# Two graph and two expert layers on one core: table work of the prologue split between VectorE and GpSimd, the count table cleared by ScalarE, weights loaded inside the first sums, narrow one-hots for the counted groups

## The chip, the cores and the metric

One core of a Trainium2 chip runs the whole program in one launch. The metric is the device time in microseconds (us); lower is better. Engines are named as the profile names them: PE (TensorE), DVE (VectorE), ACT (ScalarE), POOL (GpSimd), SP (SyncE, which only issues transfers here).

## The reference, cut to what matters

```python
n    = layernorm(x, eps=1e-5)                               # 3125 nodes x 256
# graph part of layer 0
msg  = concat(n[src], edge_attr_64) @ W_message              # 50,000 edges, 256 + 64 -> 256
agg  = segment_sum(msg, dst, 3125)
h    = layernorm(relu(agg) + n)
h    = mlp_with_skips(h, W0, W1, W2)
x    = x + layernorm(n + h)
# then: top-2 of 16 experts, a graph layer of neighbour means with top-32 of 256 kept, top-2 of 8 experts
```

The edges are sorted by `dst`, and `dst` is crowded at low nodes: about a third of the edges end in the first 350 nodes. The product with `W_message` is linear, so the kernel sums the raw rows per node first (256 features and 64 edge features) and multiplies by the weights afterwards.

## The kernel before

**Prologue** (up to the first `end_step()`, a barrier of all engines). The 3125 x 256 input comes in five pieces of five 128-row tiles (`X`); DVE takes statistics of each (L398, L402), inverts the deviation (L435, L437), ACT writes the normalized rows `NR` (L343), and SP stores them to memory as `n_rows` (L290), from where they are gathered later. The edge lists come in as `srci` and `dsti`, 98 groups of 512 edges, one group to a partition. DVE casts them to float (L406, L407) behind the third piece's statistics. When the fifth piece's statistics are done (`if p == IT`), DVE finds the smallest and largest node of each group and, for the first 33 groups, of each 128 edges (L411 to L429). `ends` holds three columns per group: first node, range, and the span of the 128-edge parts. PE turns `ends` into rows; DVE reads off two flags, `mixed_flag` and `order_flag`, which choose between a general path and the ordered path that this input takes. For the 33 dense groups ("counted" groups) DVE also makes the tables `low_i`, `high_i`, `low_f`, `rel_f`, `at_f` (L430 to L451), which PE turns into `lo_tab` and `at_tab`. POOL sets the constants, then clears `sumT` (L325, 128 x 9984) and `adj` (L326, 128 x 9800). ACT issues the eleven weight loads (L355) at its end. SP waits for all stores of `n_rows` before the barrier.

**First sums** (`sums_and_nodes("O0", ...)`). The 98 groups of 512 edges are worked from the last (`o = 0`) to the first (`o = 97`); each group's edges fall in a window of at most 128 nodes. For one group:

- `hot` (L694, DVE) writes a one-hot `O0OH`, 128 edges x 4 x 128 nodes;
- `gather` (L666, POOL, four indirect transfers) brings the `n_rows` of the source nodes, for the first `NS` = 65 groups only, into a ring of four groups;
- `products` (L685, PE) multiplies: for `o < 65` three halves (two of the node features, one of the edge features `O0EA`) by four parts of 128 edges, for the 33 counted groups only the third half;
- `add` (L707, DVE) adds the sums to `sumT` at the window's first node.

The node features of the counted groups are summed otherwise: `Adjacency` counts in `adj` how often a source node meets each of the first 384 nodes (`hot`, `count`, `add` at L731 to L753; 66 units, all of them beside the first 65 groups), and multiplies `adj` by `NR` (`piece`, L768, 20 + 20 pieces; `join`, L781) beside the counted groups.

The node stage (`NodeMlp`) runs between: nodes are worked in tiles of 128 from the last to the first, in steps `u` of a fixed plan. Each step has four places, `group(0)` to `group(3)`, at which up to four edge groups (98 groups over 30 steps) stand in both PE's and DVE's program. In PE's order a step is: transposes of `O0H` (L504), group(0), `O0ps_agg` (L1197, L1199; waits for ACT's `O0lhs`, L1161), MLP layer 0, group(1), layer 2, transposes of `O0N`, group(2), layer 1, the gate product (L1238), group(3). ACT's `O0lhs` of a step stands behind two deviations and `O0hT`, which wait for DVE's last statistics of the step before; DVE's last statistics stand behind `O0logit` (L1309), which waits for the gate product. Steps 20 to 29 hold the 33 counted groups; the tiles of the last nodes stand in steps 2 to 31.

PE, DVE and ACT each run their instructions in program order. On this ordered path PE waits for all eleven weight loads before its first product.

## Time and profile before

| what | value |
|---|---|
| median of three runs | 1650.35 us (1650.1 to 1653.77) |
| the profiled execution | 1652.82 us, its span 1651.1 us |
| PE busy / weight loads busy | 1167.3 us (71%) / 1030.7 us (62%) |
| DVE busy | 824.9 us (50%) |
| ACT busy | 413.0 us (25%) |
| POOL busy | 849.4 us (51%) |
| mean granted TensorE clock | 0.869 |

Busy shares are means over stages that differ. The prologue ends at about 44 us, the first sums and the node stage run from 47 to about 570 us; the rest of the span belongs to stages that the change does not touch. All rows below count time in us from the span's start. "x8" is the number of instructions merged into one row; one 32-bit product of the program is two MATMUL records.

### The profile page before, as it was taken

How to read it: one execution, taken by the hardware profiler on the slowest of the kernel's cores; microseconds unless marked ns; L12 is line 12 of the kernel's file. 1: busy time of each engine (PE TensorE's matmuls, PEld its weight loads, DVE VectorE, ACT ScalarE, POOL GpSimd, SP SyncE). 2: the span in 40 equal slices, each digit the busy share in tenths (PEclk: the TensorE clock that was granted, in tenths of full speed). 3: DMA queues.
4: the chain of work that ended last, by engine and by line, in shares of the span. 5: the costliest groups of instructions: out<-in, count | busy, mean ns of one | idle time of the engine just before them, and what ended most of it. 6: DMA issues, size and time to landing. Idle time of an engine off the chain costs nothing. (4 is left out here: it accounts for less than half of the span.)

```text
span 1651.1 us, 28826 instructions
## 1 busy us (share of the span) xinstructions
PE 1167.3 (71%) x7477; PEld 1030.7 (62%) x7478; DVE 824.9 (50%) x2484; ACT 413.0 (25%) x1372; POOL 849.4 (51%) x910
## 2 busy tenths in 40 slices
PE   1579898988998459999974666456666556489900
PEld 0578888888888349999971223246565555479900
DVE  7466787787768441111116999322322223644434
ACT  3001111121221223444434443000000001245533
POOL 5677776674000032222228875377777774064466
PEclk9999999999999579999996898687778887699955
DMA  5544444443112039999972321434344332034355
GB/s 182 136 132 129 126 130 114 122 125 96 42 42 59 6 124 341 354 352 349 342 256 69 87 76 53 160 106 112 112 115 114 110 109 83 21 111 129 122 164 155
DMA packets 191419, 229.78 MB, mean 139 GB/s; under 512 B 70978, under 2 KB 150868, under 8 KB 191050
## 3 DMA queue, kind: packets, MB, share of 16 engines
q1 hardware_dynamic: 153394, 129.65, 24.4%
q0 software_dynamic: 35520, 96.73, 20.9%
q10 hardware_dynamic: 2392, 2.06, 0.6%
q8 instruction: 49, 0.80, 0.2%
q14 instruction: 64, 0.52, 0.1%
HBM read 196.64 MB, written 32.04 MB: 138 GB/s over the span
## 5 line engine op out<-in xcount | busy, mean ns | idle before, releaser
L666 POOL DMA_INDIRECT O0G<-n_rows,src_tab x260 | 255.5, 983 | 119.7 <-issue 98.1
L666 POOL DMA_INDIRECT O1G<-sparse_rows,src_tab x260 | 251.3, 966 | 94.1 <-issue 90.8
L685 PE MATMUL O1ps_sums<-O1OH,O1G 128*128 128x128 f32 x1040 | 180.0, 345 | 141.0 <-issue 100.5
L685 PEld LDWEIGHTS O1ps_sums<-O1OH,O1G 128*128 128x128 f32 x1040 | 167.1, 252 | 155.3 <-issue 129.1
L1600 POOL DMA_INDIRECT e0xs<-token_rows,e0idx x64 | 60.5, 945 | 196.0 <-ACT e0idx L1669 194.9
L685 PE MATMUL O0ps_sums<-O0OH,O0G 128*128 128x128 f32 x1040 | 130.9, 280 | 31.7 <-DMA O0EA<-in_edge_attr 16.0
L685 PEld LDWEIGHTS O0ps_sums<-O0OH,O0G 128*128 128x128 f32 x1040 | 124.1, 195 | 36.1 <-issue 36.0
L707 DVE TENSOR_TENSOR sumT<-sumT,O1ps_sums 128x256 f32 x65 | 27.4, 422 | 238.7 <-PE O1ps_sums L685 238.7
L1721 DVE TENSOR_TENSOR e0ys<-e0ps_y,NR 128x256 f32<-128x256 f32 x64 | 27.2, 424 | 229.2 <-PE e0ps_y L1640 229.2
L1626 PE MATMUL e0ps_h<-e0xT,e0W 128*128 128x128 f32 x1024 | 127.9, 279 | 1.5 <-DMA e0W<-in_L_ffn_w 1.5
L1626 PEld LDWEIGHTS e0ps_h<-e0xT,e0W 128*128 128x128 f32 x1024 | 122.5, 196 | 1.9 <-DMA e0W<-in_L_ffn_w 1.9
L1640 PE MATMUL e0ps_y<-e0W,e0hidT 128*128 128x256 f32 x512 | 120.9, 379 | 0.0
L685 PE MATMUL O0ps_sums<-O0OH,O0EA 128*128 128x128 f32 x784 | 104.8, 277 | 1.6 <-DVE sumT L707 1.6
L1890 PE MATMUL m0ps_d<-m0w_dense,m0nT 128*128 128x512 f32 x100 | 63.6, 769 | 53.3 <-ACT m0nT L1858 53.3
L1600 POOL DMA_INDIRECT e1xs<-token_rows,e1idx x56 | 56.3, 1005 | 85.2 <-ACT e1idx L1669 83.5
L1640 PEld LDWEIGHTS e0ps_y<-e0W,e0hidT 128*128 128x128 f32 x512 | 92.5, 190 | 9.9
L685 PEld LDWEIGHTS O0ps_sums<-O0OH,O0EA 128*128 128x128 f32 x784 | 96.0, 193 | 2.4 <-DVE O0OH L694 2.4
L1683 ACT ACTIVATE e0hidT<-e0ps_h,b_cols 128x128 f32<-128x128 f32 x256 | 73.0, 368 | 94.6 <-PE e0ps_h L1626 94.6
L1181 PE MATMUL O0ps<-O0hT,w_mlp 128*128 128x128 f32 x600 | 87.9, 295 | 6.7 <-ACT O0hT L1154 4.8
L707 DVE TENSOR_TENSOR sumT<-sumT,O0ps_sums 128x384 f32 (+1 forms) x98 | 45.2, 461 | 91.5 <-PE O0ps_sums L685 90.5
L1383 POOL IOTA r0ii<- 128x64 int32 x1 | 0.2, 191 | 175.3 <-SPq L1341 175.3
L1181 PEld LDWEIGHTS O0ps<-O0hT,w_mlp 128*128 128x128 f32 x600 | 83.6, 210 | 9.0 <-ACT O0hT L1154 6.0
(340 smaller groups left out, 2322.7 us busy)
## 6 DMA issues: line engine op xcount, KB each, us to landing
e0W<-in_L_ffn_w SPq DMA_DIRECT2D x128, 512.0 KB, 5.8
O0EA<-in_edge_attr SPq DMA_DIRECT2D x97, 128.0 KB
expert_out<-e0ys SPq DMA_DIRECT2D x64, 128.0 KB, 5.3
expert_out<-e1ys SPq DMA_DIRECT2D x56, 128.0 KB, 1.9
O0G<-n_rows,src_tab POOLq DMA_INDIRECT x260
O1G<-sparse_rows,src_tab POOLq DMA_INDIRECT x260, 2.8
e1W_all<-in_L_ffn_w SPq DMA_DIRECT2D x16, 256.0 KB, 6.4
n_rows<-NR SPq DMA_DIRECT2D x5, 640.0 KB
```

Source lines behind the costliest of these rows:

```text
L666: pool.indirect_dma_start(out=self.G[:, s, k, :], out_offset=None, in_=self.rows_dram, in_offset=bass.IndirectOffsetOnAxis(ap=src_tab[:, g ...
L685: last = nc.tensor.matmul(self.ps[o % 2][:, half * P:(half + 1) * P], rows, self.OH[:, h, k, :], start=(k == 0), stop=(k == GC - 1))
L707: nc.vector.tensor_tensor(window, window, self.ps[o % 2][:, first * P:(first + n) * P].rearrange("p (h w) -> p h w", h=n), ALU.add).then_i ...
L1181: last = nc.tensor.matmul(ps_l[:, m * P:(m + 1) * P], w_mlp[:, l, k, m * P:(m + 1) * P], hT[:, s, k, :], start=(k == 0), stop=(k == K2 - 1))
L1383: nc.gpsimd.iota(ii[:], [[1, NB]], base=0, channel_multiplier=0)
L1600: pool.indirect_dma_start(out=xs[:, s, :], out_offset=None, in_=token_dram, in_offset=bass.IndirectOffsetOnAxis(ap=idx[:, s:s + 1], axis=0 ...
L1626: last = nc.tensor.matmul(ps_h[:, s % 2, j * P:(j + 1) * P], W1[:, s, k, j * P:(j + 1) * P], xT[:, s, k, :], start=(k == 0), stop=(k == K2 ...
L1640: last = nc.tensor.matmul(ps_y[:, s % 2, 0:D], hidT[:, s, j, :], rows, start=(j == 0), stop=(j == FJ - 1))
L1683: last = nc.scalar.activation(hidT[:, s, j, :], ps_h[:, s % 2, j * P:(j + 1) * P], func, bias=b1_cols[:, ds(e * FJ + j, 1)])
L1721: nc.vector.tensor_tensor(ys[:, s, :], ps_y[:, s % 2, 0:D], tile_of(b2_rows, e), ALU.add).then_inc(y_ready, 1)
L1890: last = nc.tensor.matmul(ps_d[:], nT[:, s, k, :], w_dense[:, k, :], start=(k == 0), stop=(k == K2 - 1))
```

## The change

1. POOL no longer clears `adj`; ACT does, with five activations of 128 x 1960 at the head of the first sums, and DVE's first addition to `adj` waits for it. POOL's clearing of `sumT` is cut into 12 pieces of 128 x 832.
2. `low_i` and `high_i` are made by DVE ahead of the minima instead of behind them; the casts to `low_f` and `at_f`, the difference `rel_f` and the sum `at_f` are made by POOL.
3. The weight loads are issued by ACT behind the clearing, in the first sums; PE and DVE wait for them at step 2 (`AHEAD`) instead of PE at the start.
4. For the 33 counted groups the one-hot has 32 nodes instead of 128, the product takes 65 columns of `O0EA` (64 features and a one) as stationary operand and 32 moving columns, and the addition covers 65 partitions x 32. A third column of `ends` now also carries each counted group's range less 24, so that a range of 32 nodes or more sets the flag of the general path; the largest range of a counted group in this input is 22.

```diff
@@ -25,6 +25,7 @@
+NARROW = 32
@@ -252,7 +253,7 @@
-            s_dn, s_tab, s_tabp = sem("dense_chain"), sem("dense_tables"), sem("dense_transposed")
+            s_dn, s_pt, s_tab, s_tabp = sem("dense_chain"), sem("dense_parts"), sem("dense_tables"), sem("dense_transposed")
@@ -322,8 +323,17 @@
-                nc.gpsimd.memset(sumT[:], 0.0)
-                nc.gpsimd.memset(adj[:], 0.0)
+                for h in range(3):
+                    for w in range(0, WIN, WIN // 4):
+                        nc.gpsimd.memset(sumT[:, h, w:w + WIN // 4], 0.0)
+                dense_dst = dstf[0:DENSE_GROUPS, :].rearrange("g (c e) -> g c e", c=GC)
+                pool.wait_ge(s_pt, 1)
+                nc.gpsimd.tensor_copy(low_f[:], low_i[:])
+                nc.gpsimd.tensor_copy(at_f[:], high_i[:]).then_inc(s_pt, 1)
+                pool.wait_ge(s_dn, 1)
+                nc.gpsimd.tensor_tensor(rel_f[:], dense_dst, tile_min[:].unsqueeze(2).to_broadcast([DENSE_GROUPS, GC, P]), ALU.subtract).then_inc(s_pt, 1)
+                pool.wait_ge(s_pt, 3)
+                nc.gpsimd.tensor_tensor(at_f[:], at_f[:], rel_f[:].rearrange("g c e -> g (c e)"), ALU.add).then_inc(s_tab, 1)
@@ -342,18 +352,6 @@
-
-                loads = [(w_nodes[:], a["L0_gnn_W_message"][0:D, :].rearrange("(k p) n -> p k n", p=P)),
-                         (w_edges[0:DE, 0:D], a["L0_gnn_W_message"][D:D + DE, :]),
-                         (gate_w0[:], a["L0_ffn_gate_w"].rearrange("(k p) n -> p k n", p=P)),
-                         (gate_b0[:], a["L0_ffn_gate_b"].rearrange("(a n) -> a n", a=1).to_broadcast([P, E0]))]
-                for l in range(3):
-                    loads.append((w_mlp[:, l, :, :], a[f"L0_gnn_mlp_W{l}"].rearrange("(k p) n -> p k n", p=P)))
-                for k, name in enumerate(LN_NAMES):
-                    loads.append((ln_rows[:, k, :], a[name].rearrange("(a n) -> a n", a=1).to_broadcast([P, D])))
-                for to, src in loads:
-                    act.dma_start(to, src).then_inc(s_w, 16)
-                assert len(loads) == N_LOADS
@@ -408,6 +406,8 @@
+                        nc.vector.tensor_scalar(low_i[:], srci[0:DENSE_GROUPS, :], P - 1, None, ALU.bitwise_and)
+                        nc.vector.tensor_scalar(high_i[:], srci[0:DENSE_GROUPS, :], 7, SPAN_BITS, ALU.arith_shift_right, ALU.logical_shift_left).then_inc(s_pt, 1)
@@ -426,9 +426,10 @@
-                        nc.vector.tensor_tensor(ends[:, 1:2], ends[:, 1:2], ends[:, 0:1], ALU.subtract).then_inc(s_end, 1)
-                        nc.vector.tensor_scalar(low_i[:], srci[0:DENSE_GROUPS, :], P - 1, None, ALU.bitwise_and)
-                        nc.vector.tensor_scalar(high_i[:], srci[0:DENSE_GROUPS, :], 7, SPAN_BITS, ALU.arith_shift_right, ALU.logical_shift_left).then_inc(s_dn, 1)
+                        nc.vector.tensor_tensor(ends[:, 1:2], ends[:, 1:2], ends[:, 0:1], ALU.subtract).then_inc(s_dn, 1)
+                        dve.wait_ge(s_dn, 4)
+                        nc.vector.scalar_tensor_tensor(ends[0:DENSE_GROUPS, 2:3], ends[0:DENSE_GROUPS, 1:2], float(NARROW - SPAN),
+                                                       ends[0:DENSE_GROUPS, 2:3], ALU.subtract, ALU.max).then_inc(s_end, 1)
@@ -439,16 +440,8 @@
-                dense_dst = dstf[0:DENSE_GROUPS, :].rearrange("g (c e) -> g c e", c=GC)
-                dve.wait_ge(s_dn, 4)
-                nc.vector.tensor_copy(low_f[:], low_i[:])
-                nc.vector.tensor_copy(at_f[:], high_i[:])
-                nc.vector.tensor_tensor(rel_f[:], dense_dst, tile_min[:].unsqueeze(2).to_broadcast([DENSE_GROUPS, GC, P]),
-                                        ALU.subtract).then_inc(s_dn, 1)
...
-                dve.wait_ge(s_dn, 5)
-                nc.vector.tensor_tensor(at_f[:], at_f[:], rel_f[:].rearrange("g c e -> g (c e)"), ALU.add).then_inc(s_tab, 1)
@@ -667,9 +660,6 @@
-            def halves_of(self, o):
-                return range(self.halves) if o < NS else range(K2, self.halves)
-
@@ -679,10 +669,15 @@
-                for half in self.halves_of(o):
+                if o < NS:
+                    for half in range(self.halves):
+                        for k in range(GC):
+                            rows = self.EA[:, e, k, :] if half == 2 else self.G[:, r, k, half * P:(half + 1) * P]
+                            last = nc.tensor.matmul(self.ps[o % 2][:, half * P:(half + 1) * P], rows, self.OH[:, h, k, :],
+                                                    start=(k == 0), stop=(k == GC - 1))
+                else:
...
-                        rows = self.EA[:, e, k, :] if half == 2 else self.G[:, r, k, half * P:(half + 1) * P]
-                        last = nc.tensor.matmul(self.ps[o % 2][:, half * P:(half + 1) * P], rows, self.OH[:, h, k, :],
+                        last = nc.tensor.matmul(self.ps[o % 2][0:DE + 1, 0:NARROW], self.EA[:, e, k, 0:DE + 1], self.OH[:, h, k, 0:NARROW],
@@ -691,9 +686,10 @@
+                w = P if o < NS else NARROW
...
-                    self.OH[:, o % HR, :, :], iota_w[:].unsqueeze(1).to_broadcast([P, GC, P]),
-                    rel_tab[:, NG - 1 - o, :].unsqueeze(2).to_broadcast([P, GC, P]),
+                    self.OH[:, o % HR, :, 0:w], iota_w[:, 0:w].unsqueeze(1).to_broadcast([P, GC, w]),
+                    rel_tab[:, NG - 1 - o, :].unsqueeze(2).to_broadcast([P, GC, w]),
@@ -702,10 +698,12 @@
-                first, n = self.halves_of(o)[0], len(self.halves_of(o))
-                window = sumT[:, first:first + n, ds(base, P)]
-                nc.vector.tensor_tensor(window, window, self.ps[o % 2][:, first * P:(first + n) * P].rearrange("p (h w) -> p h w", h=n),
-                                        ALU.add).then_inc(self.added, 1)
+                if o < NS:
+                    window = sumT[:, 0:self.halves, ds(base, P)]
+                    sums = self.ps[o % 2][:, 0:self.halves * P].rearrange("p (h w) -> p h w", h=self.halves)
+                else:
+                    window, sums = sumT[0:DE + 1, 2, ds(base, NARROW)], self.ps[o % 2][0:DE + 1, 0:NARROW]
+                nc.vector.tensor_tensor(window, window, sums, ALU.add).then_inc(self.added, 1)
@@ -716,8 +714,13 @@
-                self.hot_ready, self.counted, self.added, self.passed, self.joined = (
-                    sem(tag + "adj_" + n) for n in ("hot_ready", "counted", "added", "passed", "joined"))
+                self.cleared, self.hot_ready, self.counted, self.added, self.passed, self.joined = (
+                    sem(tag + "adj_" + n) for n in ("cleared", "hot_ready", "counted", "added", "passed", "joined"))
+
+            def clear(self, act):
+                for t in range(0, T, TU):
+                    last = nc.scalar.activation(adj[:, t:t + TU, :], ones[:, 0:1].unsqueeze(2).to_broadcast([P, TU, DW + SPAN]), ACT.Copy, scale=0.0)
+                last.then_inc(self.cleared, 1)
@@ -746,6 +749,8 @@
+                if v == 0:
+                    dve.wait_ge(self.cleared, 1)
@@ -980,6 +985,19 @@
+
+        def load_weights(act):
+            loads = [(w_edges[0:DE, 0:D], a["L0_gnn_W_message"][D:D + DE, :]),
+                     (w_nodes[:], a["L0_gnn_W_message"][0:D, :].rearrange("(k p) n -> p k n", p=P))]
+            for l in range(3):
+                loads.append((w_mlp[:, l, :, :], a[f"L0_gnn_mlp_W{l}"].rearrange("(k p) n -> p k n", p=P)))
+            for k, name in enumerate(LN_NAMES):
+                loads.append((ln_rows[:, k, :], a[name].rearrange("(a n) -> a n", a=1).to_broadcast([P, D])))
+            loads += [(gate_w0[:], a["L0_ffn_gate_w"].rearrange("(k p) n -> p k n", p=P)),
+                      (gate_b0[:], a["L0_ffn_gate_b"].rearrange("(a n) -> a n", a=1).to_broadcast([P, E0]))]
+            assert len(loads) == N_LOADS
+            for to, src in loads:
+                act.dma_start(to, src).then_inc(s_w, 16)
@@ -1063,6 +1081,9 @@
+                    if with_edges:
+                        adjacency.clear(act)
+                        load_weights(act)
@@ -1078,21 +1099,25 @@
-                    if with_edges:
-                        pe.wait_ge(s_w, 16 * N_LOADS)
...
+                        if with_edges:
+                            pe.wait_ge(s_w, 16 * N_LOADS)
...
+                            if with_edges and u == AHEAD:
+                                pe.wait_ge(s_w, 16 * N_LOADS)
...
+                        if with_edges:
+                            dve.wait_ge(s_w, 16 * N_LOADS)
@@ -1104,6 +1129,8 @@
+                            if with_edges and u == AHEAD:
+                                dve.wait_ge(s_w, 16 * N_LOADS)
```

DVE in the prologue, from the fifth piece's statistics to the flags. The names are those of the kernel's tables; before:

```order
L429 TENSOR_TENSOR ends<-ends 98x1
L430 TENSOR_SCALAR low_i<-srci 33x512
L431 TENSOR_SCALAR high_i<-srci 33x512
L435 RECIPROCAL rs<-rs 128x5
L437 SCALAR_TENSOR_TENSOR mrs<-mv,rs 128x5
L439 TENSOR_SCALAR NR<-X,mv,rs 128x256 x2
L444 CAST low_f<-low_i 33x512
L445 CAST at_f<-high_i 33x512
L446 TENSOR_TENSOR rel_f<-dstf,tile_min 33x512
L449 CAST src_tab<-ps_t 128x4x98
L451 TENSOR_TENSOR at_f<-at_f,rel_f 33x512
L453 COPY endr<-ps_e 1x294
```

The same place now:

```order
L409 TENSOR_SCALAR low_i<-srci 33x512
L410 TENSOR_SCALAR high_i<-srci 33x512
L411 TENSOR_SCALAR dlow<-dstf 98x512
...
L429 TENSOR_TENSOR ends<-ends 98x1
L431 SCALAR_TENSOR_TENSOR ends<-ends 33x1
L436 RECIPROCAL rs<-rs 128x5
L438 SCALAR_TENSOR_TENSOR mrs<-mv,rs 128x5
L440 TENSOR_SCALAR NR<-X,mv,rs 128x256 x2
L444 CAST src_tab<-ps_t 128x4x98
L446 COPY endr<-ps_e 1x294
```

Two instructions have moved ahead, one small one on `ends` is new, and four are gone from DVE. They stand on POOL now, whose last instructions before the barrier are these, where it had only `MEMSET sumT 128x9984` and `MEMSET adj 128x9800` behind `iota_at`:

```order
L325 CAST iota_at<-iota_ai 128x200
L328 MEMSET sumT 128x832 x12
L331 CAST low_f<-low_i 33x512
L332 CAST at_f<-high_i 33x512
L334 TENSOR_TENSOR rel_f<-dstf,tile_min 33x512
L336 TENSOR_TENSOR at_f<-at_f,rel_f 33x512
```

PE in the first sums, the end of one step and the start of the next, with two counted groups (`O0EA`) in it; before:

```order
L504 MATMUL O0ps_turned<-ident,O0N 128x128 x2
L685 MATMUL O0ps_sums<-O0OH,O0EA 128x128 x4
L768 MATMUL O0ps_adj<-adj,NR 128x256 x5
L1181 MATMUL O0ps_1<-O0hT,w_mlp 128x128 x4
L1238 MATMUL O0ps_back<-gate_w,O0nT 128x16 x2
L504 MATMUL O0ps_turned<-ident,O0H 128x128 x2
L685 MATMUL O0ps_sums<-O0OH,O0EA 128x128 x4
L768 MATMUL O0ps_adj<-adj,NR 128x256 x5
L1197 MATMUL O0ps_agg<-w_edges,O0lhs 128x257
```

and now:

```order
L497 MATMUL O0ps_turned<-ident,O0N 128x128 x2
L680 MATMUL O0ps_sums<-O0OH,O0EA 65x32 x4
L773 MATMUL O0ps_adj<-adj,NR 128x256 x5
L1208 MATMUL O0ps_1<-O0hT,w_mlp 128x128 x4
L1265 MATMUL O0ps_back<-gate_w,O0nT 128x16 x2
L497 MATMUL O0ps_turned<-ident,O0H 128x128 x2
L680 MATMUL O0ps_sums<-O0OH,O0EA 65x32 x4
L773 MATMUL O0ps_adj<-adj,NR 128x256 x5
L1224 MATMUL O0ps_agg<-w_edges,O0lhs 128x257
```

Nothing has moved there; the four products of a counted group have another shape.

## Rows read from the trace of the kernel before

**Rows 1.** Windows: PE, PEld, DVE, ACT, POOL busy us (x instructions), PEclk, DMA share, GB/s

```profile
60.00:80.00 20.00, 17.91 (x137) 17.32 (x135) 12.81 (x29) 0.00 (x0) 15.26 (x16) 1.00 0.51 134
420.00:440.00 20.00, 17.23 (x115) 15.44 (x114) 15.56 (x59) 4.98 (x16) 0.00 (x0) 1.00 0.19 47
```

**Rows 2.** Timeline, DVE, prologue: start us, duration us, engine, line, operation

```profile
13.09 0.45 DVE L402 BATCH_NORM_AGGREGATE mv<-st 128x2 f32<-128x6 f32 x5
13.45 10.22 DVE L406 CAST srcf<-srci 98x512 f32<-98x512 int32 x1
23.59 0.41 DVE L407 CAST dstf<-dsti 98x512 f32<-98x512 int32 x1
```

**Rows 3.** Timeline, POOL, prologue

```profile
6.77 8.42 POOL L325 MEMSET sumT<- 128x9984 f32 x1
15.13 8.27 POOL L326 MEMSET adj<- 128x9800 f32 x1
```

**Rows 4.** Transfers of 0 to 30 us: busy tenths in 40 slices of 0.75 us

```profile
DMA  0054599999999999999992000000000000000896
```

**Rows 5.** Timeline, DVE, end of the prologue

```profile
36.05 0.41 DVE L444 CAST low_f<-low_i 33x512 f32<-33x512 int32 x1
...
37.32 0.83 DVE L449 CAST src_tab<-ps_t 128x392 int32<-128x392 f32 x1
38.00 0.68 DVE L451 TENSOR_TENSOR at_f<-at_f,rel_f 33x512 f32<-33x512 f32 x1
```

**Rows 6.** Waits of SP's queue, 36 to 64 us: total us, times, longest

```profile
SPq L212 <- DMA n_rows<-NR: 4.4, 1, 4.4
...
SPq L212 <- PEq L212: 1.6, 1, 1.6
```

**Rows 7.** Groups of POOL by form: xcount | busy us, mean ns | idle before

```profile
L666 POOL DMA_INDIRECT O0G<-n_rows,src_tab x260 | 255.5, 983 | 119.7 <-issue 98.1 <-PE O0ps_sums L685 21.7
...
L1781 POOL TENSOR_TENSOR m0H<-m0Y,m0own 128x256 f32<-128x256 f32 x25 | 21.7, 868 | 2.0 <-ACT m0Y L1774 1.4
```

**Rows 8.** Groups of ACT by form

```profile
L1161 ACT ACTIVATE O0lhs<-sumT 128x384 f32<-128x384 f32 x25 | 12.8, 513 | 53.6 <-DVE sumT L707 53.6
```

**Rows 9.** Timelines at the start of the first sums: PE, then DVE

```profile
58.88 3.75 PE L685 MATMUL O0ps_sums<-O0OH,O0G 128*128 128x128 f32 x16 [16.04 <-DMA O0EA<-in_edge_attr]
...
65.15 0.86 DVE L753 TENSOR_TENSOR adj<-adj,O0ps_adj 128x200 f32 x2
```

**Rows 10.** Timeline, PE, one step of the counted groups

```profile
453.27 0.60 PE L1197 MATMUL O0ps_agg<-w_edges,O0lhs 65*128 65x257 f32 x2
...
463.79 0.52 PE L1238 MATMUL O0ps_back<-gate_w,O0nT 128*128 128x16 f32 x4
...
464.41 1.06 PE L685 MATMUL O0ps_sums<-O0OH,O0EA 128*128 128x128 f32 x8
465.30 2.32 PE L768 MATMUL O0ps_adj<-adj,NR 128*128 128x256 f32 x10
467.46 0.60 PE L1197 MATMUL O0ps_agg<-w_edges,O0lhs 65*128 65x257 f32 x2
```

**Rows 11.** Timeline, weight loads (PEld) of the prologue: stationary rows*columns, here 33*1

```profile
40.11 0.08 PEld L379 LDWEIGHTS ps_a<-ident,tile_min 33*1 33x1 f32 x2
```

**Rows 12.** Groups of DVE by form, whole span

```profile
L694 DVE TENSOR_TENSOR O0OH<-iota_w,rel_tab 128x512 f32<-128x512 f32 x98 | 66.5, 679 | 0.0
...
L707 DVE TENSOR_TENSOR sumT<-sumT,O0ps_sums 128x128 f32 x33 | 9.4, 284 | 20.4 <-PE O0ps_sums L685 19.7 <-DVE sumT L707 0.5
...
L1309 DVE TENSOR_TENSOR O0logit<-O0ps_back,gate_b 128x16 f32<-128x16 f32 x25 | 4.2, 168 | 4.5 <-PE O0ps_back L1238 4.5
```

**Rows 13.** Timeline, ACT, the same step

```profile
466.66 0.51 ACT L1161 ACTIVATE O0lhs<-sumT 128x384 f32<-128x384 f32 x1
```

**Rows 14.** Timeline, PE, around a wait of 2.79 us

```profile
481.40 0.70 PE L1197 MATMUL O0ps_agg<-w_edges,O0lhs 65*128 65x257 f32 x2 [2.79 <-ACT O0lhs L1161]
...
483.59 1.91 PE L1181 MATMUL O0ps<-O0hT,w_mlp 128*128 128x128 f32 x8
```

## The prediction

> **What bounds the kernel now.** I read the windows first, then the timelines of the two places that the change touches, then the waits and the groups by form. In the windows [rows 1] the first sums show two regimes. At 60 to 80 us POOL is busy 15.26 of 20 us and goes from one indirect transfer to the next: 983 ns each and about 0.29 us of issue between them (98.1 us over 260, less one gap of 23.8 at the start) [rows 7], so 5.1 us for a group of four. That pace, with PE close behind, sets the time of the first 65 groups. From 420 us POOL is idle and PE is busy 17.23 of 20 us, DVE 15.56: PE's order bounds, with a chain through DVE and ACT nearly as long. In the prologue one row stands out: DVE's cast of `srci` lasts 10.22 us, the same cast of `dsti` behind it 0.41 us [rows 2]. It ends at 23.67, right behind POOL's clearing of `adj` (15.13 + 8.27 = 23.40) [rows 3]. The input has been in since about 16.5 us, where the transfers stop [rows 4], so DVE's statistics of pieces four and five wait for the cast and nothing else.
>
> **The cast and POOL's clearing.** The row shows that this cast stands still while POOL clears. It did not get in at 15.13 either, where one clearing ended and the next began. So I take it that back-to-back clearings keep it out, and that it now ends 0.27 us behind the last piece of `sumT`: 15.19 plus a little for twelve instructions instead of one (0.2 us), instead of 23.40. That is 8.0 us earlier. The other bound: it slips in behind the piece that runs at 13.45 (0.7 us each) and ends near 14.4, so that DVE is 9.2 us earlier. The fourth and fifth pieces of the input do not stop it: they are there by 16.5 us [rows 4], and the fifth is wanted at 19.
>
> The Trainium skill (SBUF — State Buffer, "two separate sides") says that VectorE in a two-port mode and GpSimd take one shared pair of ports exclusively, for a whole instruction. The 10.22 us agree, and by "whole instruction" the twelve pieces would let the cast in at 14.2, 9.2 us of gain; the boundary at 15.13 speaks against it, and the sum goes by the row.
>
> **The table work.** Gone from DVE behind the fifth piece: 36.05 to 37.32 (two casts and `rel_f`) and the 0.6 us of `at_f` [rows 5], 1.9 us. `low_i` and `high_i` only change places ahead of the same reciprocal. One small instruction with its wait is new in the chain to `ends`: 0.25 us. SP had its stores landed 1.6 us before the last engine came [rows 6], and SP's stores do not gain from the shorter tail; so of 1.9 us only 1.6 counts, and SP then sets the barrier. On POOL the two casts and two two-input operations cost at most 0.87 us per 256 elements [rows 7], under 2 us each for 512; they start when `high_i` is done and end some 5 us later, while PE wants them only behind `ends`, the row of bases and its broadcast, more than 4 us later: no wait. But they run beside DVE's `dlow`, its two-input sum and the last normalizing, and what held up the cast can hold these up too, each for at most one POOL instruction. Bounds: 0 and 2.5 us; I take 1.2, about one such wait. Prologue: 8.0 + 1.6 - 0.25 - 1.2 = **8.2 us**; between 5.5 and 10.6.
>
> **Clearing and weights in the first sums.** ACT's 128x384 takes 513 ns [rows 8], so 1960 elements take at most 2.6 us and five of them 13. ACT has nothing else to do there; they end before 50 us, and DVE's first addition to `adj`, now at 65.15 [rows 9], then comes near 57. The eleven loads (1.65 MB) go out by 50 us, and at the 134 GB/s of a window with gathers [rows 1] need 12 us; they are wanted at step 2, after seven groups of 5.1 us, near 75 us. Both cost nothing. If that cover were gone, PE could be late by 4 us before POOL's ring of four groups stops: PE's first product is at 58.88 [rows 9], waiting for `O0EA` and not for weights, so the removed wait gives nothing either. What starts 8.2 us earlier stays 8.2 us earlier through the 65 groups, as every wait in them is relative to the start.
>
> **The counted groups.** PE: 464.41 to 465.30 is one group, 0.89 us [rows 10], or 0.111 per record at eight records. Fewer moving columns alone do not help: from 463.79, four records with 16 moving columns and two transposes take 0.62 us [rows 10], 0.10 each, so the stationary load of 128 columns sets that pitch. With one column, two loads take 0.08 us together [rows 11]. For 65 columns I take half of 0.111, so 0.45 per group and 0.44 saved; bounds 0.04 (pitch 0.10) and 0.65 (pitch 0.03). The Trainium skill (TensorE: Matmul & The Clock Gate, "LDWEIGHTS") gives columns / 1.2 ns, 54 ns for 65 columns: an estimate from it of 0.43 per group and 0.46 saved, near my value. DVE: 679 + 284 ns per group now [rows 12]; after it 128 elements at about 0.28 (the 128x128 row) and 32 at about 0.19 (the 128x16 row takes 0.168), so 0.49 saved.
>
> How much of it is on the path? A step lasts 467.46 - 453.27 = 14.19 us, and PE has no idle time in it [rows 10]. From `O0ps_agg` to the gate product PE runs through with two groups inside: 2 x 0.44 come off fully. From the gate product to the next `O0ps_agg` are 3.67 us, but the chain gate product, `O0logit`, statistics, deviation, `O0hT`, `O0lhs` ends at 466.66 + 0.51 = 467.17 [rows 13], so only 0.3 us of the 0.44 comes off there. Some 1.15 us per step, and steps 20 to 24 give 5.7. In steps 25 to 27, where three to four groups stand and DVE's group(3) lies ahead of `O0logit`, both engines' savings shorten that chain: 1.4 each, 4.2. In steps 28 and 29 DVE runs without a pause and PE waits for its additions: seven groups at 0.49, 3.4. Sum **13.3 us** of the 14.5 that all 33 groups would give PE. Bounds: DVE's part alone, 5; all at the best pitch, 33 x 0.65 = 21.
>
> **Sum.** 8.2 + 13.3 = 21.5 us. The profiled execution took 1652.82 us, so it would be 1631.3; the median of the runs lies 2.5 below it, and I subtract from that: 1650.35 - 21.5 = **1629**.
>
> **Rivals.**
> - The load does not follow the columns: pitch stays 0.10, PE's step stays as long, and only DVE's shorter chain helps, 5 us. For it: the 16-column row shows that nothing but the load matters; against it: the one-column loads. 1650.35 - 13.2 = 1637. Chance 0.17.
> - Everything is on the path: the cast slips in, no contention, SP's stores land sooner as no weights stand beside them (10.6), and a group saves 0.6 (19): 1621. For it: steps where PE waits for `O0lhs` may shorten with DVE. Chance 0.13.
> - The prologue gives only 2 us, as POOL's table work and DVE's minima hold each other up at each instruction and PE waits for `s_tab`: 15.3 in all, 1635. For it: the 10.22 us show how complete such a stop is; against it: each POOL instruction is short. Chance 0.12.
> - Slower: TensorE's clock. Behind a wait of 2.79 us PE runs eight 128x128 records in 1.91 us instead of 1.06 [rows 10, 14]; the first is the level of 1.2 GHz, the other of 2.4. PE has less to do per step now and so idles at `O0lhs`. One such spell lasts about 4 us and costs 1.6. It decides once more than 13 spells stand in ten steps, or some 21 us of PE's work runs at the low level: 1655 if it is 25 us. Against it: only one of the waits shown fell so, and the new ones are under 1 us. Chance 0.04.
> - The change does not do what it says: the range less 24 sets the flag and the general path is taken, far slower. The largest range is 22 against 32. Chance 0.01. Or all savings vanish in waits: within 5 us, 0.03.
>
> **How the numbers follow.** My forecast has 0.50, with 1624 to 1634 as its own range. Leaving out the slow cases and half of the fastest, the range goes from 1619 to 1639: the low end is 10.6 + 20, the high end 5.5 + 6. A measurement tells about 0.3%, 5 us. Faster holds the forecast and the first three rivals, 0.92; the same 0.04; slower 0.04.
>
> **What would show it.** Right: the cast of `srci` under 2.5 us and ending near 15.5; the first gather at 39 instead of 47; last clearing of `adj` before 50; the counted products at eight records in 0.45 us and steps near 13 us. Wrong: DVE operations of over 1 us beside POOL's table work; PE waiting for a weight load; the narrow records at a pitch of 0.10; more rows of 1.9 us for eight records; longer waits for `O0lhs` at an unchanged step.

## The result

| | before | changed kernel |
|---|---|---|
| median of 5 runs each (lowest, highest) | 1653.45 us (1650.1, 1653.81) | 1638.38 us (1636.04, 1642.24) |
| span and granted clock of the profiled run | 1651.1 us, 0.869 | 1636.6 us, 0.870 |

The ratio of the means is 0.9919, with a 95% interval of 0.990 to 0.9938: faster by 13.4 us (10 to 16.5); the two medians lie 15.1 us apart. The prediction said 21.5 us. Against the 1650.35 us from which it was subtracted, the changed kernel is 12.0 lower; its 1638.4 is 9.4 above the forecast, above the forecast's own range of 1624 to 1634 and just inside the upper end of the wide one.

**The prologue.** The timeline of the changed kernel, VectorE (DVE) and GpSimd (POOL), against [rows 2, 3, 5]:

```profile
13.62 0.80 DVE L404 CAST srcf<-srci 98x512 f32<-98x512 int32 x1
14.35 1.09 DVE L405 CAST dstf<-dsti 98x512 f32<-98x512 int32 x1
...
22.87 0.74 POOL L331 CAST low_f<-low_i 33x512 f32<-33x512 int32 x1 [6.71 <-DVE high_i L410]
23.56 1.84 POOL L332 CAST at_f<-high_i 33x512 f32<-33x512 int32 x1
24.25 0.67 DVE L415 TENSOR_TENSOR dlow<-dlow,dstf 98x512 f32<-98x512 f32 x1
24.85 0.56 DVE L417 TENSOR_TENSOR tile_span<-tile_max,tile_min 33x4 f32<-33x4 f32 x1
25.37 1.03 POOL L334 TENSOR_TENSOR rel_f<-dstf,tile_min 33x512 f32<-33x512 f32 x1
26.48 1.25 POOL L336 TENSOR_TENSOR at_f<-at_f,rel_f 33x512 f32<-33x512 f32 x1
26.53 1.23 DVE L423 SCALAR_TENSOR_TENSOR tile_span<-tile_max,tile_span 33x4 f32<-33x4 f32 x1
```

The 10.22 us of the first cast have become 0.80. Both casts got in between the clearing's pieces and end at 15.44; before, at 24.00. Then look at the two `tile_span` rows: 33x4 elements, 0.14 to 0.15 us where POOL is quiet (the runs below), here 0.56 and 1.23, and each ends where a POOL instruction ends. That is the contention that was priced at 1.2; it cost 1.5. POOL pays too: `at_f` takes 1.84 us, `low_f`, the same cast beside VectorE operations of one input, 0.74. VectorE's two-input `dlow` came 0.7 us behind the start of `at_f` and still took the 0.67 us that it took before.

SP's waits from 28 to 60 us, against [rows 6], and the start of the first sums, against [rows 9]:

```profile
SPq L213 <- DMA n_rows<-NR: 2.9, 1, 2.9
SPq L213 <- PEq L213: 1.3, 1, 1.3
```

```profile
35.58 1.83 ACT L722 ACTIVATE adj<-ones 128x1960 f32<-128x1960 f32 x1 [5.46 <-PEq L146]
...
37.96 1.21 POOL L659 DMA_INDIRECT O0G<-n_rows,src_tab  x1 [10.22 <-issue]
...
42.19 22.40 SPq L652 DMA_DIRECT2D O0EA<-in_edge_attr  x6
...
51.62 3.75 PE L676 MATMUL O0ps_sums<-O0OH,O0G 128*128 128x128 f32 x16 [17.63 <-DMA O0EA<-in_edge_attr]
```

The first gather starts 9.2 us earlier (37.96, was 47.18). The first product starts only 7.3 earlier: its edge rows, issued at 42.19, land 9.4 us later, beside the eleven weight loads; before they took 4.3. The next readings show what that is worth.

**Where the time went, by landmarks** (start times in the two traces, us):

| | before | after | earlier by |
|---|---|---|---|
| first gather | 47.2 | 38.0 | 9.2 |
| last product of the gathered groups | 416.6 | 404.8 | 11.8 |
| last `O0ps_agg` record (end of the counted groups) | 542.6 | 523.0 | 19.6 |
| last gather of `o1Y` | 1641.3 | 1626.8 | 14.5 |

The counted groups give 7.8 (19.6 less 11.8), and 5.1 us are lost again (19.6 less 14.5; the expectations below have 5.2) in stages that the change does not touch. The runs below deal with both.

**The counted groups.** One step of the changed kernel on TensorE (PE) and ScalarE (ACT), against [rows 10, 13], and the groups of VectorE by form, against [rows 12]:

```profile
446.10 2.40 PE L773 MATMUL O0ps_adj<-adj,NR 128*128 128x256 f32 x10
448.34 1.05 PE L1208 MATMUL O0ps<-O0hT,w_mlp 128*128 128x128 f32 x8
449.23 0.52 PE L1265 MATMUL O0ps_back<-gate_w,O0nT 128*128 128x16 f32 x4
449.85 0.61 PE L680 MATMUL O0ps_sums<-O0OH,O0EA 128*65 128x32 f32 x8
450.29 2.40 PE L773 MATMUL O0ps_adj<-adj,NR 128*128 128x256 f32 x10
452.11 0.51 ACT L1188 ACTIVATE O0lhs<-sumT 128x384 f32<-128x384 f32 x1
452.67 0.70 PE L1224 MATMUL O0ps_agg<-w_edges,O0lhs 65*128 65x257 f32 x2
```

```profile
L690 DVE TENSOR_TENSOR O0OH<-iota_w,rel_tab 128x128 f32<-128x128 f32 x33 | 9.2, 279 | 0.0
L706 DVE TENSOR_TENSOR sumT<-sumT,O0ps_sums 65x32 f32 x33 | 6.0, 182 | 27.0 <-PE O0ps_sums L680 24.4 <-issue 1.7 <-DVE sumT L706 0.6
```

From 449.85 to 450.29 is one group: 0.44 us for eight records, 0.055 each (0.45 was forecast). VectorE takes 279 and 182 ns (0.28 and 0.19). So both savings of a group are as sized. But the ten big products behind such a group now take 2.24 us (446.10 to 448.34; in [rows 10] 465.30 to 467.46, 2.16): 0.08 of the 0.44 goes back. And PE starts `O0ps_agg` right where ACT's `O0lhs` ends (452.62). The step is closed by the chain now, no longer by PE.

The starts of `O0ps_agg` give the steps: 13.67, 14.30, 14.19, 13.94 us before, 12.48, 13.33, 13.32, 13.52 after. The stretch before the first is 10.42 in both, closed by a wait for `O0lhs` of 2.33 and 2.34.

The last of these steps, and the eight records behind it, against [rows 14]:

```profile
466.19 0.70 PE L1224 MATMUL O0ps_agg<-w_edges,O0lhs 65*128 65x257 f32 x2 [3.29 <-ACT O0lhs L1188]
...
468.56 1.92 PE L1208 MATMUL O0ps<-O0hT,w_mlp 128*128 128x128 f32 x8
```

The wait of 2.79 us has grown to 3.29: PE gets to it 0.92 us sooner (10.23 us behind the start of the step, was 11.15), and the step gains 0.42. The eight records behind it take 1.92 us, at the level of 1.2 GHz as before (1.91). The end of the counted groups, in windows as in [rows 1] and in the timeline:

```profile
500.00:510.00 10.00, 6.22 (x60) 5.47 (x59) 7.77 (x33) 0.97 (x3) 0.00 (x0) 0.90 0.35 86
510.00:515.00 5.00, 3.34 (x22) 2.85 (x22) 2.77 (x15) 0.72 (x3) 0.00 (x0) 0.50 0.20 69
```

```profile
507.10 0.64 PE L680 MATMUL O0ps_sums<-O0OH,O0EA 128*65 128x32 f32 x8
508.12 0.18 DVE L706 TENSOR_TENSOR sumT<-sumT,O0ps_sums 65x32 f32 x1 [0.52 <-PE O0ps_sums L680]
508.45 1.06 PE L680 MATMUL O0ps_sums<-O0OH,O0EA 128*65 128x32 f32 x8 [0.71 <-DVE sumT L706]
508.81 0.48 DVE L1329 SCALAR_TENSOR_TENSOR O0Z<-O0Z,O0nzrs,ln_rows 128x256 f32<-128x256 f32 x1
509.21 0.28 DVE L690 TENSOR_TENSOR O0OH<-iota_w,rel_tab 128x128 f32<-128x128 f32 x1
509.68 0.18 DVE L706 TENSOR_TENSOR sumT<-sumT,O0ps_sums 65x32 f32 x1 [0.18 <-PE O0ps_sums L680]
```

Neither engine is full here: the two rows that wait name each other, addition behind product, product behind addition. And the clock falls from 2.4 to 1.2 GHz between two groups: the one at 508.45 takes 1.06 us, the one at 507.10 took 0.64. The same two groups in the kernel before, at full clock:

```profile
527.05 0.29 DVE L707 TENSOR_TENSOR sumT<-sumT,O0ps_sums 128x128 f32 x1
...
527.49 1.13 PE L685 MATMUL O0ps_sums<-O0OH,O0EA 128*128 128x128 f32 x8 [0.31 <-DVE sumT L707]
...
528.25 0.69 DVE L694 TENSOR_TENSOR O0OH<-iota_w,rel_tab 128x512 f32<-128x512 f32 x1
528.85 0.28 DVE L707 TENSOR_TENSOR sumT<-sumT,O0ps_sums 128x128 f32 x1
```

From addition to addition 1.80 us before and 1.56 after: 0.24 gained, where 0.49 was forecast.

How much of the loss stands at full clock can be read off. A mark that lies alike in both kernels, ahead of the last seven additions, is this row, the changed kernel first:

```profile
502.29 0.41 PE L1235 MATMUL O0ps_back<-ident,O0hT 128*128 128x128 f32 x2 [1.23 <-DVE O0logit L1336]
```

```profile
521.08 0.41 PE L1208 MATMUL O0ps_back<-ident,O0hT 128*128 128x128 f32 x2 [0.84 <-DVE O0logit L1309]
```

| stretch | before | after | gained | forecast |
|---|---|---|---|---|
| `O0ps_agg` of the step above to this mark (steps 25 to 27 and the head of 28) | 39.68 | 36.10 | 3.58 | 4.2 |
| the mark to the product at 527.49 (508.45 after): three additions, full clock in both | 6.41 | 6.16 | 0.25 | 1.5 |
| from there to the next `O0ps_agg`: four additions, low clock after, full for the most part before | 7.70 | 7.08 | 0.62 | 2.0 |

So 1.8 of the 3.2 us that are missing in these five steps are lost where the clock is alike in both.

### The profile page after: what moved, and what is told of

Its sections match the earlier page's. It is cut to its first block and busy times, and to the rows that moved or that the text cites. A ratio compares the mean times of both kernels' runs of the same rounds, so it can differ in the third digit from the quotient of the medians.

```text
span 1636.6 us, 28844 instructions
## 1 busy us (share of the span) xinstructions
PE 1155.9 (71%) x7477; PEld 1022.2 (62%) x7478; DVE 798.7 (49%) x2481; ACT 422.1 (26%) x1377; POOL 854.1 (52%) x924
## 5 line engine op out<-in xcount | busy, mean ns | idle before, releaser
L659 POOL DMA_INDIRECT O0G<-n_rows,src_tab x260 | 259.7, 999 | 99.4 <-issue 84.8
L659 POOL DMA_INDIRECT O1G<-sparse_rows,src_tab x260 | 254.6, 979 | 94.1 <-issue 92.0
L706 DVE TENSOR_TENSOR sumT<-sumT,O0ps_sums 128x384 f32 (+1 forms) x98 | 41.8, 427 | 98.1 <-PE O0ps_sums L676 70.6
L2019 ACT ACTIVATE O1lhs<-sumT 128x256 f32<-128x256 f32 x25 | 10.4, 415 | 258.9 <-DVE sumT L706 258.9
L676 PE MATMUL O0ps_sums<-O0OH,O0EA 128*128 128x128 f32 x520 | 70.8, 280 | 0.0
```

The source lines that it names most:

```text
L659: pool.indirect_dma_start(out=self.G[:, s, k, :], out_offset=None, in_=self.rows_dram, in_offset=bass.IndirectOffsetOnAxis(ap=src_tab[:, g ...
L676: last = nc.tensor.matmul(self.ps[o % 2][:, half * P:(half + 1) * P], rows, self.OH[:, h, k, :], start=(k == 0), stop=(k == GC - 1))
L706: nc.vector.tensor_tensor(window, window, sums, ALU.add).then_inc(self.added, 1)
L2019: nc.scalar.activation(self.lhs[:, s, :, :], sumT[:, 0:K2, ds(node_tile(t) * P, P)], ACT.Copy).then_inc(S["lhs_ready"], 1)
```

## The experiments

They ran on three chips. On two of them the gathered phase takes some 433 us instead of 369, in every kernel, so medians compare only within a job; each ratio is to the kernel before in the same job.

| run | kernel before | this, median (runs) | ratio, 95% interval | first gather | gathered | counted | behind |
|---|---|---|---|---|---|---|---|
| before_again | 1776.51 | 1776.52 (1) | | 47.2 | 433.1 | 127.5 | 1153.9 |
| after_again | 1772.69 | 1760.18 (4) | 0.9920, 0.9895 to 0.9945 | 38.8 | 433.3 | 118.1 | 1155.9 |
| wide_hots | 1772.69 | 1767.10 (9) | 0.9962, 0.9947 to 0.9977 | 38.8 | 432.5 | 127.5 | 1153.5 |
| narrow_only | 1772.69 | 1769.25 (10) | 0.9974, 0.9961 to 0.9987 | 47.4 | 432.6 | 119.9 | 1154.6 |
| adj_by_act | 1772.69 | 1765.64 (10) | 0.9956, 0.9940 to 0.9973 | 39.0 | 428.7 | 127.6 | 1155.4 |
| cols128_moving32 | 1776.51 | 1764.02 (4) | 0.9929, 0.9907 to 0.9951 | 38.8 | 433.2 | 122.6 | 1156.4 |
| pool_waits_ends | 1776.51 | 1760.10 (4) | 0.9905, 0.9884 to 0.9925 | 39.5 | 434.6 | 118.2 | 1155.7 |
| weights_early | 1776.51 | 1760.81 (4) | 0.9905, 0.9884 to 0.9925 | 39.6 | 435.7 | 118.2 | 1153.4 |
| two_parts | 1656.91 | 1642.29 (6) | 0.9922, 0.9898 to 0.9946 | 39.2 | 370.5 | 118.2 | 1100.2 |
| cols65_moving128 | 1656.91 | 1647.83 (9) | 0.9955, 0.9940 to 0.9971 | 38.8 | 365.8 | 125.9 | 1102.7 |
| whole_clear | 1656.91 | 1639.00 (4) | 0.9915, 0.9886 to 0.9943 | 38.8 | 368.3 | 118.2 | 1099.8 |

"Gathered" runs from the first gather to the last product of the gathered groups, "counted" from there to the last `O0ps_agg`, "behind" to the last gather of `o1Y`. For the first pair of traces these are 369.4, 126.0 and 1098.7 before, 366.8, 118.2 and 1103.8 after. Every kernel has the same work in the first and the last of them, and they scatter by 7 and by 3 to 5 us. "Counted" and the first gather are what to read. "Counted" repeats to 0.2 us where the code is the same, with one exception: the kernels with wide products say 127.5 on the two slower chips and 126.0 on the others, and narrow_only 119.9 where the changed kernel says 118.1. It lies in one step, behind the first wait of 2.33 us for `O0lhs`. before_again, then the same place in after_again:

```profile
489.00:494.00 5.00, 4.94 (x24) 4.60 (x25) 1.68 (x4) 0.63 (x3) 0.00 (x0) 0.66 0.00 0
491.11 1.92 PE L1181 MATMUL O0ps<-O0hT,w_mlp 128*128 128x128 f32 x8
```

```profile
482.45 1.06 PE L1208 MATMUL O0ps<-O0hT,w_mlp 128*128 128x128 f32 x8
```

The clock fell to 1.2 GHz for some 4 us there, and the step takes 15.31 us instead of the 13.67 of the first trace. before_again, wide_hots, adj_by_act and narrow_only (14.11 instead of 12.48) have this spell, the nine other traces do not, though the wait ahead of it is 2.33 to 2.35 us in all. So 1.6 us must come off a comparison of a trace that has it with one that has not.

**wide_hots**: the changed kernel without its fourth part.

```
-  matmul(ps[0:DE+1, 0:NARROW], EA[:, e, k, 0:DE+1], OH[:, h, k, 0:NARROW])
+  matmul(ps[:, 2*P:3*P],       EA[:, e, k, :],      OH[:, h, k, :])
```

> The change without its fourth part: one-hots of 128 nodes, 128 stationary and 128 moving columns for the counted groups; prologue, clearing by ScalarE and weight loads as changed. Theory A (the parts add, and what is missing of my sum after the first sums is scatter of stages that the change does not touch): first gather at 38.0 us as in the changed kernel, last counted group to the aggregate product of the last-but-one tile 115 us behind the first counted group as before, total 9 us under the kernel before, give or take 3. Theory B (the change loses some 5 us in later stages by itself): total only 4 us under before.

(These texts count the stage from the first counted group to the last `O0ps_agg` but one, 115.4 us in the first trace of before.) The counted stage is back at 127.5, the value of before_again, spell and all. The rest of the change alone has the first gather at 38.8 and a gain of 6.7 us.

**narrow_only**: the other half, the kernel before with the narrow groups alone (the same lines the other way round, and the `ends` term).

> The kernel before with the fourth part alone. Theory A: first gather at 47 us, counted stage 107.5 us instead of 115.4, total 8 us under the kernel before. Rival (the counted stage gives the 13.3 us of my sum and the changed kernel lost some of it to something else, such as the clock): counted stage 102 us, total 13 under.

The stage takes 119.9 us, 7.6 less than the 127.5, with the spell in both; the ratio says 4.6 us (2.3 to 6.9), less than the 8 expected. Both are far below 13.3.

**adj_by_act**: the kernel before with the clearing of `adj` alone moved to ACT.

```
-  nc.gpsimd.memset(adj[:], 0.0)
+  for t in range(0, T, TU): activation(adj[:, t:t+TU, :], ones, Copy, scale=0.0)   # ACT, first sums
```

> The kernel before, where ScalarE clears the count table at the head of the first sums and GpSimd does not; the clearing of sumT stays one instruction, the table work stays on VectorE, the weights are loaded in the prologue. Theory (the cast waits for the GpSimd instruction that runs): the cast of srci ends at 15.5 us instead of 23.7, VectorE's last prologue instruction at 35.3 instead of 43.5, first gather near 39.5, total 7.5 us under before. Rival (the move of the weights and the table work are what frees the prologue): first gather later than 44, total within 3 us of before.

VectorE's rows of this run:

```profile
13.17 2.29 DVE L405 CAST srcf<-srci 98x512 f32<-98x512 int32 x1
...
35.10 0.22 DVE L486 COPY gate_w<-ps_w 128x8 f32<-128x8 f32 x2
```

`sumT` is cleared in one instruction of 8.42 us here, and the cast ends behind it, at 15.46. The first gather comes at 39.0, 8.2 us earlier than before: one moved line gives all of the prologue that was forecast, and all but 0.2 of what the changed kernel shows in the same job. The later rows say why the split of the table adds nothing. VectorE's last row of the prologue ends at 35.32 here. In after_again, without the two casts, `rel_f` and the sum of `at_f`, it ends at about the same time:

```profile
13.71 2.19 DVE L404 CAST srcf<-srci 98x512 f32<-98x512 int32 x1
...
27.36 1.23 DVE L423 SCALAR_TENSOR_TENSOR tile_span<-tile_max,tile_span 33x4 f32<-33x4 f32 x1
...
35.27 0.22 DVE L480 COPY gate_w<-ps_w 128x8 f32<-128x8 f32 x2
```

**after_again**, **before_again**: both kernels once more.

> The changed kernel once more, with its own profile. Theory A: the gain up to the aggregate products of the last tiles is 19 to 20 us again, and the loss behind them is another number than the 5.2 us of the first profile, anywhere from -2 to +6; total 11 to 17 us under before. Theory B: the loss behind them is 5 us again, within 1.

> The kernel before once more, for a second profile. If the stages behind the first sums scatter by themselves (theory A), the time from the last aggregate product (L1199) to the last gather of the last sums differs from the changed kernel's on the same chip by another amount than the 5.2 us of the first pair, with either sign; if the change costs something there (theory B), it is 4 to 6 us shorter than in the changed kernel again.

The stages behind differ by 2.0 us here, not by 5.1, though the two traces are of two chips, where the text asks for one; other kernels fall on both sides of this pair. The 5.1 is no more than what traces of the same work scatter by (3 to 5 us, above). The 9.4 us between the counted stages (127.5 and 118.1) are 7.8 and the spell of 1.6. A small systematic loss is not excluded: the traces of the other kernels lie 1.1 (seven on the slower chips) and 2.9 us (four on the faster ones) above the single trace of before, on average.

**pool_waits_ends**: POOL's `rel_f` waits until VectorE has made `ends`, so that the two no longer run beside each other there.

```
-  pool.wait_ge(s_dn, 1)
+  pool.wait_ge(s_end, 1)
```

> The changed kernel, but GpSimd makes rel_f and the sum at_f only when VectorE has finished the ends (one wait on another semaphore). Theory (two-input VectorE operations and GpSimd's table work hold each other up): tile_span takes 0.15 us in both places instead of 0.56 and 1.23, VectorE's last prologue instruction ends 1.3 to 1.5 us earlier, GpSimd's at_f still ends before TensorE's transposes want it at 31; first gather 1 us earlier, total -1. Rival: the hold-up only moves to the last normalizing (L440) and the cast of src_tab, last instruction where it was.

```profile
25.66 0.56 DVE L417 TENSOR_TENSOR tile_span<-tile_max,tile_min 33x4 f32<-33x4 f32 x1
27.33 0.14 DVE L423 SCALAR_TENSOR_TENSOR tile_span<-tile_max,tile_span 33x4 f32<-33x4 f32 x1
...
29.04 1.67 DVE L440 TENSOR_SCALAR NR<-X,mv,rs 128x256 f32<-128x256 f32 x2
```

The second `tile_span` is down from 1.23 to 0.14 us, which shows that the 1.23 was POOL's doing. But the stop only moves: `NR`, 0.73 us elsewhere, takes 1.67 beside POOL's later table work, and the first gather is at 39.5, 0.7 later than in after_again. The ratio (0.9905) is not to be told from that of the changed kernel.

**weights_early**: the changed kernel with the weights issued at the end of ACT's prologue, as before the change.

```
   last.then_inc(s_na, 1)
+  load_weights(act)                 # end of ACT's prologue
...
-  load_weights(act)                 # start of the first sums
```

> The changed kernel with the weight loads issued at the end of ScalarE's prologue again, the waits left at step 2. Theory (the loads beside the first gathers only use a cover): VectorE's first memset of the first sums 1.5 us later (its code is fetched beside the loads), O0EA lands 2 to 4 us earlier and the first product starts at 49 to 50 instead of 51.6 us, the 16th gather 1.5 to 2.5 us earlier relative to the first, end of the 65 groups unchanged within the scatter of 3 us, total within 3. Rival (the late weights cost time that stays): total 3 to 5 us less.

SP's waits and the first product:

```profile
SPq L213 <- DMA n_rows<-NR: 5.1, 1, 5.1
```

```profile
48.88 3.33 PE L687 MATMUL O0ps_sums<-O0OH,O0G 128*128 128x128 f32 x14 [14.85 <-DMA O0EA<-in_edge_attr]
```

Beside the weights the stores of `NR` land later (a wait of 5.1 us, 2.9 in the changed kernel) and the first gather comes 0.8 later than in after_again; in exchange the first product comes 3 us earlier. The two traces differ in the cast too: here it got in between the pieces, as in the first trace of the changed kernel, and against that one (37.96) the first gather is 1.6 later. VectorE's first memset comes 2.4 us later than in after_again (1.5 expected), and the 16th gather comes 19.8 us behind the first, against 19.2 and 19.9 in the two traces of the changed kernel, so the 1.5 to 2.5 us expected there do not show. The whole tells no difference: 0.9905 and 0.9920, within the intervals. That the ring of four groups covers a late first product, as forecast, agrees with this.

**cols128_moving32**: the changed kernel, counted products with 128 stationary columns and 32 moving ones. **cols65_moving128**: the reverse, and VectorE makes and adds the wide windows (65 partitions x 128). The addition of the first stays at 65 partitions x 32, not the 128 of its text.

```
   matmul(ps[0:DE+1, 0:NARROW], EA[:, e, k, 0:DE+1], OH[:, h, k, 0:NARROW])   # changed kernel
   matmul(ps[:, 0:NARROW],      EA[:, e, k, :],      OH[:, h, k, 0:NARROW])   # cols128_moving32
   matmul(ps[0:DE+1, 0:P],      EA[:, e, k, 0:DE+1], OH[:, h, k, :])          # cols65_moving128
```

> The changed kernel, but the counted products keep 128 stationary columns; 32 moving columns, narrow one-hot and narrow addition (128 partitions) stay. Theory (the stationary load sets the pitch, and the chain through VectorE and ScalarE sets more than half of the step): a group takes 0.89 us again, the stage from the first counted group to the last aggregate product is some 5 us longer than in the changed kernel, total +5. Rival (moving columns set it): a group takes 0.45 us or less, total unchanged. Second rival (VectorE's shorter work gave nothing): the stage is 8 us longer, as long as before.

> The changed kernel with 65 stationary columns but one-hots over 128 nodes again for the counted groups, so VectorE makes and adds the wide windows. Theory A (a record takes the longer of its load and its product, and the product of 128 nodes takes as long as the load of 128 columns): eight products in 0.89 us, VectorE 0.68 and 0.28 us, the stage near 127.5 as with everything wide. Theory B (the record's time is set by the stationary columns alone): eight in 0.44 us, and the stage near 122.5, the VectorE half of the gain missing only.

One group of each, and the big products behind it:

```profile
475.20 0.98 PE L680 MATMUL O0ps_sums<-O0OH,O0EA 128*128 128x32 f32 x8
476.01 2.40 PE L773 MATMUL O0ps_adj<-adj,NR 128*128 128x256 f32 x10
```

```profile
415.85 1.04 PE L680 MATMUL O0ps_sums<-O0OH,O0EA 128*65 128x128 f32 x8
416.72 2.33 PE L773 MATMUL O0ps_adj<-adj,NR 128*128 128x256 f32 x10
```

128 stationary and 32 moving columns: 0.81 us to the next row, 0.10 a record; 65 and 128: 0.87. Only both narrow give 0.44. The four figures fit a record that takes the longer of its load and its product, and either alone saves PE next to nothing. The stage says 122.6 for the first and 125.9 for the second, which gains nothing (126.0 before). The first has no spell of low clock in its first step, so it compares with 126.0: VectorE's saving alone gives 3.4 us of the 7.8. By steps, it gives 0.5 of the 3.45 in the four steps whose starts are listed above and 3.0 of the 4.4 in the five behind; the rest needs PE's saving. The second row of each shows when the 0.08 is paid: 2.40 behind the groups with 32 moving columns in both kernels that have them, 2.33 behind wide ones.

The clock at the end of the stage is best compared in windows that lie alike before its end (13 to 8 us ahead of the last `O0ps_agg`). The kernel before, then cols65_moving128; the answering window of the changed kernel is the second of those shown above (510 to 515), at 0.50:

```profile
529.60:534.60 5.00, 3.02 (x22) 2.62 (x20) 3.11 (x13) 0.68 (x2) 0.00 (x0) 0.90 0.16 56
```

```profile
517.50:522.50 5.00, 2.96 (x19) 2.51 (x17) 2.99 (x13) 0.72 (x3) 0.00 (x0) 0.85 0.12 41
```

In this window all five traces with wide moving columns (those two, before_again, wide_hots, adj_by_act) show 0.85 to 0.97, and all eight with 32 moving columns 0.50, cols128_moving32 too, whose groups keep PE as long as before. The clock falls at the end of the stage in every kernel; with 32 moving columns it falls some 5 us sooner. Why is not shown: PE is busy for 3.3 us of this window in the changed kernel, for 4.3 in cols128_moving32 and for 3.0 in the kernel before.

**two_parts**: the kernel before with the two parts that gave something, adj_by_act and narrow_only.

> The kernel before with two parts of the change alone: adj cleared by ScalarE, and the counted groups over 32 nodes and 65 columns. The table work stays on VectorE and the weights in the prologue, as before. Theory A (these two parts are all of it; the split of the table and the later weights are worth nothing): first gather near 39, the stage of the counted groups 118, and 0.990 to 0.992 of the time before, as the whole change had. Theory B (the gains of the parts run alone, 0.9974 and 0.9956, simply add, and the other two parts carry the rest): 0.993, 3 us behind the whole change.

0.9922, and 118.2 us for the stage: the whole gain within what can be told. The split of the table and the later weights are worth nothing measurable, one way or the other. That they might carry 3 us together is what this run makes unlikely, though its interval does not exclude it.

**whole_clear**: the changed kernel with `sumT` cleared in one instruction.

```
-  for h in range(3):
-      for w in range(0, WIN, WIN // 4): nc.gpsimd.memset(sumT[:, h, w:w + WIN // 4], 0.0)
+  nc.gpsimd.memset(sumT[:], 0.0)
```

> The changed kernel with sumT cleared in one instruction of GpSimd instead of twelve. Theory A (VectorE's cast of srci either waits for the clearing to end or slips between pieces, and what it gains there is lost in the tables behind): the cast of srci takes 2.2 to 2.3 us and ends near 15.5, the first gather starts at 38.5 to 39.5, the whole as the changed kernel within 2 us. Theory B (the pieces are worth their slip): first gather 1 us later than 38.8 and the whole 1 to 2 us longer.

The cast takes 2.10 us and ends at 15.46; first gather 38.8, and the ratio of the changed kernel. VectorE's last row of the prologue ends at 35.06, 0.4 ahead of after_again, and the first gather comes no earlier for it; what holds it is not shown. The twelve pieces gain nothing: of the seven traces with pieces the cast got in between them in two (0.80 and 0.70 us) and stood until their end in five (2.15 to 2.63).

## Why the prediction came out too high

- **What bounds the kernel**: right for the prologue and the gathered groups. The cast was the whole of the first stop, and the gathered groups kept their lead: the ratio of adj_by_act says 7.8 us (4.8 to 10.6) for 8.2 at the first gather.
- **The cast, 8.0 us**: right, 8.2 with the clearing of `adj` alone moved. The step "back-to-back clearings keep it out" held in five traces of seven and failed in the first and in weights_early, where the other bound (9.2 at the first gather of the first trace) is met. By the rule of the Trainium skill (SBUF — State Buffer, "SBUF: two separate sides") that the pair is taken for a whole instruction, the gaps between pieces should let it in, as the prediction read it; the traces show both, and a gap decides it only sometimes.
- **The table, 1.6 - 0.25 - 1.2**: right in sum (0.15 forecast; the first gather of after_again is 0.2 ahead of that of adj_by_act, its last row of VectorE 0.2 behind) and in kind: the contention is 1.5 us (1.2 forecast), at the two `tile_span` rows.
- **Clearing and weights at nothing**: right. ACT ends its five at 44.3 (1.73 apart, not 2.6), VectorE's first addition to `adj` comes at 58.7 (57 forecast), and weights_early moves landmarks at the start and not the end, as far as its interval tells.
- **The counted groups, 13.3 us**: this is the step that failed, the one on how much of a group's saving is on the path. The stage gave 7.8 us in the first pair of traces and as much later, once the spell of low clock is taken off. Both savings of a group were sized right, to 0.01 us. What was too high is the share on the path, in three places. The sum counted five steps at 1.15 from step 20; the first gave 0, since it is closed by `O0lhs` (a wait of 2.33 us that stood in the trace of before), and the four behind it 1.19, 0.97, 0.87 and 0.42, in all 3.45 of 5.7. The 0.42 is the step that ends in the wait of [rows 14], 2.79 us for `O0lhs` before the change already; the prediction read that wait for the clock and not for the path. In these steps 0.08 of each 0.44 goes back to the next big product, and once PE's own work is done before the chain through the additions and `O0lhs`, that chain closes the step. The last five steps gave 4.4 of 7.6. The term for the last two, seven groups at 0.49, is the worst of the sum: 0.87 us of 3.4. It had VectorE busy without a pause and PE behind it; now each group's product and addition wait for each other. Three of these groups gave 0.25 of 1.5 us at full clock in both kernels. For the four others, 0.62 of 2.0, the clock falls some 5 us sooner, and how their loss splits between the chain and the clock has not been measured; narrow groups at 0.64 and at 1.06 us are the only price seen.
- **The rivals**: "the load does not follow the columns" is false for both narrow together (0.055 a record), and true for 32 moving columns with 128 stationary. The estimate of 54 ns from the Trainium skill (TensorE: Matmul & The Clock Gate, "LDWEIGHTS (loading the stationary operand)") agrees with the 0.055 us of a record; cols65_moving128, with the same load and 128 moving columns, takes 0.109, so the load sets a record's time only when the moving side is as short. The clock as a rival was right in kind (longer waits, a lower level sooner at the end) and a far smaller size than 25 us.
- **The baseline**: the 1650.35 lies 3.1 us below the median of before in the job of the result. The forecast leaned on the lower of the two figures and so was lower by as much.

Prologue 8.2 to 9.2 and counted groups 7.8 make 16 to 17; the ratio says 13.4 (10 to 16.5), the medians 15.1. Up to 16.5 these lie inside the interval, and what stands behind the counted groups does not tell it from a small loss there.

## What to carry to other kernels

Look in the timeline for a small VectorE instruction that lasts as long as a GpSimd one beside it: moving the GpSimd work to an engine with nothing to do was the whole gain of the prologue here; cutting it in pieces and sharing VectorE's work with GpSimd gave nothing, as the stop came back elsewhere. Count a saving only up to the next chain that closes the step: write down for each step by how much the second chain trails (0.3 us here), look for steps that already end in a wait (the one of 2.33 us here took the saving whole, the one of 2.79 more than half), and cap each term there. To shorten a small fp32 product, narrow the stationary and the moving side together, and run each half alone: here VectorE's shorter operations gave 3.4 of the 7.8 us by themselves. Before two traces are compared, look for a spell of low clock that only one of them has.

## What the runs showed of the hardware

- In fp32 one record takes 0.055 us with 65 stationary and 32 moving columns, 0.10 with 128 and 32, 0.109 with 65 and 128, 0.111 with both at 128.
- The ten products of 256 moving columns behind a group with 32 moving columns take 2.24 us instead of 2.16, with 65 stationary columns and with 128.
- GpSimd is held up by VectorE too: the cast of 33x512 takes 0.74 us beside VectorE's operations of one input and 1.84 where a two-input one (98x512) started 0.7 us behind it; VectorE's operation kept its 0.67.
- Whether a waiting VectorE cast gets in between back-to-back clearings of GpSimd is not settled by the gaps: 0.70 and 0.80 us in two traces, 2.15 to 2.63 in five.
- Behind the same wait of 2.33 us the granted clock fell for some 4 us in four traces (0.66 over 5 us in before_again) and stayed at 1.00 in others, in the same code; a spell cost 1.6 us.
- At the end of the stage TensorE's granted clock fell to half some 5 us sooner with 32 moving columns, whatever the stationary side: 0.50 in eight traces, 0.85 to 0.97 in the same window of the five others.
